# Expert stage: table entries read into registers in half turns inside the turn

## The chip, the cores and the metric

The kernel runs on one NeuronCore of a Trainium2 chip. The metric is the device time of one execution in microseconds (us); lower is better.

## The reference, cut to what matters

A two-layer block over 4 sequences of 512 rows of width 512. Layer 0 is a scan-based mixer and a Hadamard-rotated feed-forward layer; layer 1 is masked attention over a context of 1024 rows and then the part that matters here, a mixture of experts: each of the 2048 rows goes to the 8 best of 32 experts, and each expert is a gated feed-forward layer of inner width 192.

```python
router_logits = x2d @ gate_kernel                       # (2048, 32)
routing_weights = softmax(router_logits)
routing_weights, selected_experts = top_k(routing_weights, 8)
routing_weights = routing_weights / sum(routing_weights)
# for each expert e and the rows that chose it:
y = (silu(rows @ gate_proj[e]) * (rows @ up_proj[e])) @ down_proj[e]
# added to the row of the output, times its routing weight
```

## The kernel before

The earlier stages (mixer, feed-forward, attention, router) are straight code and loops that the change doesn't touch. The router sorts the rows by expert into a table in DRAM (`rows_by_expert`), each expert's rows padded to whole tiles of 128. That gives `NTILE` = 159 tiles. Which expert a tile belongs to is known only on the chip, so DVE computes an integer table `TAB` in SBUF, one column for each tile: row 0 is the tile's expert, row 1 the value at which its expert's rows are complete (`due`), row 2 the offset of its weights in the buffer `we`, row 3 its first row in `rows_by_expert`, row 4 the first tile of its expert.

The expert stage then runs over the tiles, one after the other, on five engines at once. It is written as a hardware loop `Fori` of `LOOPS` = 19 turns with `U` = 8 tiles unrolled in each, and a rest of 7 tiles (`REST`). For a tile t:

- ACT issues the gather of the tile's rows (`load_tile`, line 793, its DMA on line 798), `LEAD` = 6 tiles ahead, into one of 8 buffers.
- PE transposes the rows, two tiles ahead (`tile_transpose`, line 1698); ACT copies the high half (`tile_hi`, line 774, activation on line 777) and DVE computes the low half (`tile_lo`, line 1371).
- PE multiplies by gate and up, one tile ahead (`tile_up`, line 1708, twelve matmuls on lines 1471 to 1473); ACT takes the silu (`tile_silu`, line 779), DVE the product (`hidden`, lines 1382 and 1383).
- PE transposes the hidden rows (`hidden_transpose`, lines 1716 and 1717); ACT copies their high half (`hidden_hi`, line 783, activation on line 785), DVE the low half (`hidden_lo`, line 1378).
- PE multiplies by the down weights (`tile_down`, line 1719); DVE weighs the result (`weigh`, lines 1390 and 1391) and POOL adds it to the output by an indirect DMA (line 568). SP loads the experts' weights.

In each tile PE's order is: transposes of tile t+2, hidden transposes of t, gate and up of t+1, down of t. ACT's is: `hidden_hi(t)`, `tile_hi(t+2)`, the gather's DMA, `tile_silu(t+1)`. DVE's is: `hidden_lo(t)`, `tile_lo(t+2)`, `hidden(t+1)`, `weigh(t)`.

An address or a semaphore value that comes from the table must stand in a register of the engine that uses it. `load_ints` (line 92) takes fresh registers, fills them with one load instruction of the engine's own queue (line 95, TENSOR_LOAD in the trace) and turns them into values. Each engine does so at the top of a turn, right behind the loop's branch:

- PE: 12 entries of row 2 (line 1735).
- ACT: 12 entries of row 3, then 16 entries of row 1 (line 811), ahead of the first `hidden_hi`.
- DVE: 8 entries of row 0 (line 1397), ahead of the first `hidden_lo`.
- POOL: 8 entries of row 4, which the change leaves as it is.

Ahead of the loop and ahead of the rest each engine loads once more in the same way.

Of the kernel before, what the change touches and what calls it, by code (L numbers as in the profile page):

```python
# [22 lines left out]
P = 128  # L23
# [6 lines left out]
NE, M, TOPK = 32, 192, 8  # L30
# [5 lines left out]
E16 = EW + EL  # L36
# [6 lines left out]
CAP = NTOK + P  # L43
SPARES = 4
WP = 4
U = 8
LEAD = 6
V = U
LOOPS = NTILE // U
REST = NTILE - LOOPS * U  # L50
NEWTON = 13
# [40 lines left out]
def load_ints(eng, name, table, least, most):  # L92

    regs = [eng.alloc_register(f"{name}{i}") for i in range(table.shape[-1])]
    eng.reg_load(regs, table)  # L95
    return [eng.snap(x, donate=True, min_val=least, max_val=most) for x in regs]


def wait_apart(eng, sem, value, passed):
# [6 lines left out]
def build(nc, a_x, a_ctxT, a_ctxr, a_kv, a_mask, a_winT, a_woutT, a_cols, a_rows, a_wug, a_wdT,  # L106
          a_gk, a_exp, a_ident, a_had, a_hadf, a_tri, d_exp, d_kv, d_row, d_down, a_out):
    ctx = ExitStack()
    with ctx:
# [3 lines left out]
        def sem(name):  # L113
            return ctx.enter_context(nc.semaphore(name))
# [131 lines left out]
        o += U * RW  # L246
        yt = [BIG[:, o + i * D:o + (i + 1) * D] for i in range(V)]
        o += V * D
        xh = [f16(BIG, o + i * D // 2, (KC, P)) for i in range(2)]
# [22 lines left out]
        TAB = ex(5 * TABLE, I32, p=1).rearrange("p (a t) -> p a t", a=5)  # L272
        TCUM = ex(NE, I32, p=1)
        TODD = ex(TABLE, I32, p=1)
        TPAD = ex(NE, I32, p=1)
        IDY = ex(V, I32)

# [51 lines left out]
        s_xg = [sem(f"tile_gathered{i}") for i in range(U)]  # L329
        s_add = [sem(f"tile_added{i}") for i in range(V)]  # L330
        s_xt, s_xh, s_xl, s_ug, s_es, s_ea, s_at, s_ah2, s_al2, s_ed, s_y = (sem(n) for n in (
# [7 lines left out]
        def _(sp):  # L339
# [156 lines left out]
            with sp.Fori(1, NE // WP) as i:  # L496
                for h in range(WP):
# [5 lines left out]
                    load_expert(i * WP + h, h)  # L503
            for w in range(V):
                sp.wait_ge(s_add[w], 16 + 16 * (LOOPS + (w < REST)))


        @block.gpsimd
        def _(pool):
# [4 lines left out]
            pool.memset(SELS[:, :], 0.0).then_inc(s_ss, 1)  # L514
            for w in range(V):
                pool.dma_start(first[:, 2 * w:2 * w + 2], a_x[0:1, 2 * w:2 * w + 2]).then_inc(s_add[w], 16)
# [53 lines left out]

            with pool.Fori(0, LOOPS) as it:
                start = load_ints(pool, "expert_start", TAB[0:1, 4, bass.ds(it * U, U)], 0, NTILE)
# [3 lines left out]
            for u in range(REST):  # L576
                add(LOOPS * U + u, u, start[u])


        @block.scalar  # L580
        def _(act):
# [192 lines left out]
            def tile_hi(t, p, weights):  # L774
                act.wait_ge(s_wl, weights)
                act.wait_ge(s_xt, t + 1)
                act.activation(xh[p], PS[:, p, :].rearrange("p (k n) -> p k n", n=P), ACT.Copy, scale=H_S).then_inc(s_xh, 1)  # L777

            def tile_silu(t, p):
                act.wait_ge(s_ug, t + 1)  # L780
                act.activation(eg[p], PS[:, 2 + p, 0:M], ACT.Silu, scale=1.0 / (H_S * E_S)).then_inc(s_es, 1)  # L781

            def hidden_hi(t, p):
                act.wait_ge(s_at, t + 1)
                act.activation(eah[p], PS[:, 4, 0:2 * P], ACT.Copy).then_inc(s_ah2, 1)  # L785

            def rows_at(name, t, count):
                return load_ints(act, name, TAB[0:1, 3, bass.ds(t, count)], 0, NE * CAP + (SPARES - 1) * P)

            def experts_due(name, t, count):  # L790
                return load_ints(act, name, TAB[0:1, 1, bass.ds(t, count)], 16, 16 * NE)

            def load_tile(u, used, row, pads):

                act.wait_ge(s_pad, pads)
                if not isinstance(used, int) or used:
                    act.wait_ge(s_y, used)
                act.dma_start(xg[u], d_row[bass.ds(row, P), :]).then_inc(s_xg[u], 16)

            act.wait_ge(s_tab, 1)  # L800
            rows, due = rows_at("first_row", 0, U), experts_due("first_due", 0, U)
# [4 lines left out]
                load_tile(t, 0, rows[t], due[t])  # L806
            tile_hi(0, 0, due[0])
            tile_hi(1, 1, due[1])
            tile_silu(0, 0)
            with act.Fori(0, LOOPS) as it:  # L810
                rows, due = rows_at("tile_row", it * U + 4, U + 4), experts_due("tile_due", it * U, U + 8)
                for u in range(U):
                    t = it * U + u

                    hidden_hi(t, u % 2)
                    tile_hi(t + 2, u % 2, due[u + 2])
                    load_tile((u + LEAD) % U, t + (V + LEAD - U + 1), rows[u + LEAD - 4], due[u + LEAD])
                    tile_silu(t + 1, (u + 1) % 2)
            t = LOOPS * U
            rows, due = rows_at("last_row", t + LEAD, REST - LEAD), experts_due("last_due", t + 2, REST - 2)  # L820
            for u in range(REST):
                hidden_hi(t + u, u % 2)
                if u + 2 < REST:
# [8 lines left out]
        def _(dve):  # L832
# [538 lines left out]
            def tile_lo(t, p):  # L1371
                dve.wait_ge(s_xh, t + 1)
                v.scalar_tensor_tensor(xl[p], PS[:, p, :].rearrange("p (k n) -> p k n", n=P), H_S, xh[p],  # L1373
                                       ALU.mult, ALU.subtract).then_inc(s_xl, 1)
# [5 lines left out]
            def hidden(t, p):  # L1380
                dve.wait_ge(s_es, t + 1)
                v.scalar_tensor_tensor(ea[p][:, 0:M], PS[:, 2 + p, M:2 * M], 1.0 / (H_S * E_S), eg[p], ALU.mult, ALU.mult)  # L1382
                v.scalar_tensor_tensor(ea[p][:, M:2 * P], PS[:, 2 + p, M + P:2 * M], 1.0 / (H_S * E_S), eg[p][:, P:M],
                                       ALU.mult, ALU.mult).then_inc(s_ea, 1)
# [9 lines left out]
            tile_lo(1, 1)  # L1394
            hidden(0, 0)
            with dve.Fori(0, LOOPS) as it:
                experts = load_ints(dve, "tile_expert", TAB[0:1, 0, bass.ds(it * U, U)], 0, NE - 1)
                for u in range(U):
                    t = it * U + u
                    hidden_lo(t, u % 2)  # L1400
                    tile_lo(t + 2, u % 2)
                    hidden(t + 1, (u + 1) % 2)
                    weigh(t, u, it * (U // V) + u // V, experts[u])
            experts = load_ints(dve, "last_expert", TAB[0:1, 0, bass.ds(LOOPS * U, REST)], 0, NE - 1)
            for u in range(REST):
                t = LOOPS * U + u
                hidden_lo(t, u % 2)
                if u + 2 < REST:
                    tile_lo(t + 2, u % 2)
                if u + 1 < REST:  # L1410
                    hidden(t + 1, (u + 1) % 2)
                weigh(t, u, LOOPS * (U // V) + u // V, experts[u])
# [3 lines left out]
        def _(pe):  # L1416
# [287 lines left out]
            def weights_at(name, t, count):  # L1704

                return load_ints(pe, name, TAB[0:1, 2, bass.ds(t, count)], 0, (WP - 1) * E16)

            def tile_up(t, p, at):
                for k in range(KC):
                    hi = we[:, bass.ds(at + k * GU, GU)]  # L1710
                    lo = we[:, bass.ds(at + (EW + k * GU), GU)]
                    last = three(PS[:, 2 + p, 0:GU], xh[p][:, k, :], xl[p][:, k, :], hi, lo, k == 0, k == KC - 1)
                last.then_inc(s_ug, 1)
# [5 lines left out]
            def tile_down(t, p, at):  # L1719
                pe.wait_ge(s_al2, t + 1)  # L1720
                bank = PS[:, 5 + p, :]
                w0h, w1 = KC * GU, KC * GU + D
                hi, lo = we[:, bass.ds(at + w0h, D)], we[:, bass.ds(at + (EW + w0h), D)]
                stack = we[:, bass.ds(at + w1, D)]
                three(bank, eah[p][:, 0:P], eal[p][:, 0:P], hi, lo, True, False)

                mm(bank, eah[p][:, P:2 * P], stack, start=False, stop=False)  # L1727
                mm(bank, eal[p][:, P:2 * P], stack, start=False, stop=True).then_inc(s_ed, 1)  # L1728
# [1 line left out]
            tile_transpose(0, 0, 0)  # L1730
            tile_transpose(1, 1, 0)
            pe.wait_ge(s_xl, 1)
            tile_up(0, 0, weights_at("first_weights", 0, 4)[0])
            with pe.Fori(0, LOOPS) as it:
                at = weights_at("tile_weights", it * U, U + 4)
                for u in range(U):
                    t = it * U + u
                    tile_transpose(t + 2, (u + 2) % U, it + (u + 2) // U)


                    pe.wait_ge(s_ea, t + 1)
                    hidden_transpose(u % 2)
                    tile_up(t + 1, (u + 1) % 2, at[u + 1])
                    tile_down(t, u % 2, at[u])
            at = weights_at("last_weights", LOOPS * U, REST)
            for u in range(REST):
                t = LOOPS * U + u
                if u + 2 < REST:
                    tile_transpose(t + 2, (u + 2) % U, LOOPS + (u + 2) // U)
                pe.wait_ge(s_ea, t + 1)  # L1750
                hidden_transpose(u % 2)
                if u + 1 < REST:
                    tile_up(t + 1, (u + 1) % 2, at[u + 1])
                tile_down(t, u % 2, at[u])


# [66 lines left out]
```

## Time and profile before

| what | us |
|---|---|
| median of 3 runs (lowest, highest) | 1517.9 (1516.97, 1525.52) |
| the profiled execution | 1522.04 |
| its span, first to last instruction | 1520.2 |

The profiled execution lies 4.1 us above the median of the runs; 1.8 us of it are around the span. The trace gives times from the start of the span. An engine's name with a q behind it (ACTq, PEldq) is its instruction queue: loads into registers, branches, copies of registers, DMA issues. PE is the matmuls and PEld the loads of their weights, which overlap. Releasers are inferred, and an engine that isn't the bottleneck may be idle at no cost.

### The profile page before, as it was taken

How to read it: one execution, taken by the hardware profiler on the slowest of the kernel's cores; microseconds unless marked ns; L12 is line 12 of the kernel's file. 1: busy time of each engine (PE TensorE's matmuls, PEld its weight loads, DVE VectorE, ACT ScalarE, POOL GpSimd, SP SyncE). 2: the span in 40 equal slices, each digit the busy share in tenths (PEclk: the TensorE clock that was granted, in tenths of full speed). 3: DMA queues.
4: the chain of work that ended last, by engine and by line, in shares of the span. 5: the costliest groups of instructions: out<-in, count | busy, mean ns of one | idle time of the engine just before them, and what ended most of it. 6: DMA issues, size and time to landing. Idle time of an engine off the chain costs nothing.

```text
span 1520.2 us, 26971 instructions
## 1 busy us (share of the span) xinstructions
PE 1397.6 (92%) x7525; PEld 757.6 (50%) x7526; DVE 1026.8 (68%) x2471; ACT 505.1 (33%) x916; POOL 382.9 (25%) x313
## 2 busy tenths in 40 slices
PE   4599999999999999988989729999999999999997
PEld 3234444444444444444444315666666666666664
DVE  6848866985896546577776645666666666666664
ACT  1335444435334343332222103333333333333332
POOL 1000000000000000014546452344443334444443
PEclk9789999999999999999999959999999999999999
DMA  9955676767666678717665757889999989999886
GB/s 369 395 188 179 229 252 225 232 206 240 205 225 218 225 257 279 274 59 274 222 219 205 288 223 195 215 223 240 250 246 230 230 219 225 254 227 225 158 160 91
DMA packets 132696, 345.04 MB, mean 227 GB/s; under 512 B 15008, under 2 KB 19616, under 8 KB 125728
## 3 DMA queue, kind: packets, MB, share of 16 engines
q1 hardware_dynamic: 74528, 208.82, 40.8%
q0 software_dynamic: 34640, 85.74, 24.7%
q10 hardware_dynamic: 23472, 49.79, 10.3%
q8 instruction: 27, 0.44, 0.1%
q14 instruction: 29, 0.24, 0.0%
HBM read 192.68 MB, written 151.62 MB: 226 GB/s over the span
## 4 chain that ended last, share of the span: by engine, by line
PE 69%; DVE 12%; DMA 6%; issue 5%; another core or an unknown queue 3%; ACT 2%; SPq 2%; ACTq 1%; DVEq 0%; POOLq 0%
PE PS L1471 18%; PE PS L1473 18%; PE PS L1472 17%; PE PS L1701 4%; PE PS L1728 2%; PE PS L1727 2%; DMA split_experts<-HT 2%; DMA CST<-in_kv 2%; PE PS L1716 1%; PE PS L1717 1%; DMA BIG<-in_wdT 1%; PE PS L1429 1%; ACTq L95 1%; PE PS L1432 1%
## 5 line engine op out<-in xcount | busy, mean ns | idle before, releaser
L568 POOL DMA_INDIRECT out<-BIG,EX x159 | 247.1, 1554 | 360.9 <-DVE BIG L1391 185.2
L1471 PE MATMUL PS<-BIG 128*128 x795 | 268.3, 338 | 4.8 <-DVE BIG L1378 3.1
L1472 PE MATMUL PS<-BIG 128*128 x795 | 268.2, 337 | 0.0
L1473 PE MATMUL PS<-BIG 128*128 x795 | 268.2, 337 | 0.0
L1471 PE MATMUL PS<-HT,BIG 128*128 128x512 f16 (+1 forms) x512 | 196.6, 384 | 4.2 <-ACT EX L621 2.3
L1472 PE MATMUL PS<-HT,BIG 128*128 128x512 f16 (+1 forms) x512 | 196.1, 383 | 0.0
L1473 PE MATMUL PS<-HT,BIG 128*128 128x512 f16 (+1 forms) x512 | 196.0, 383 | 0.0
L546 POOL DMA_INDIRECT rows_by_expert<-HT,POS x128 | 124.3, 971 | 142.9 <-DVE POS L1276 108.4
L1471 PE MATMUL PS<-BIG,EX 128*128 128x512 f16 (+1 forms) x384 | 146.3, 381 | 6.6 <-DVE EX L1218 5.0
L1472 PE MATMUL PS<-BIG,EX 128*128 128x512 f16 (+1 forms) x384 | 146.2, 381 | 0.0
L1473 PE MATMUL PS<-BIG,EX 128*128 128x512 f16 (+1 forms) x384 | 146.0, 380 | 0.0
L785 ACT ACTIVATE BIG<-PS 128x256 f16<-128x256 f32 x159 | 60.9, 383 | 245.1 <-PE PS L1717 223.6
L1382 DVE SCALAR_TENSOR_TENSOR BIG<-PS,BIG 128x192 f32<-128x192 f32 x159 | 56.8, 357 | 104.4 <-ACT BIG L781 97.7
L1373 DVE SCALAR_TENSOR_TENSOR BIG<-PS,BIG 128x512 f16<-128x512 f32 x159 | 110.0, 692 | 21.1 <-ACT BIG L777 11.1
L1391 DVE TENSOR_SCALAR BIG<-PS,BIG 128x512 f32<-128x512 f32 x159 | 119.4, 751 | 0.0
L631 ACT ACTIVATE HT<-HT 128x1280 f16<-128x1280 f32 x64 | 81.1, 1268 | 97.3 <-DMA split_experts<-HT 97.3
L1701 PE MATMUL PS<-ident,BIG 128*128 128x128 f32 x636 | 96.7, 275 | 15.6 <-DMA BIG<-rows_by_expert 14.1
L540 POOL MEMSET HT<- 128x105 f32 x1 | 0.2, 185 | 425.9 <-DMA split_experts<-HT 425.9
L1473 PEld LDWEIGHTS PS<-BIG 128*128 128x128 f16 x795 | 78.0, 98 | 58.5 <-issue 0.3
L781 ACT ACTIVATE BIG<-PS 128x192 f32<-128x192 f32 x159 | 52.5, 330 | 158.1 <-PE PS L1473 133.3
L1701 PEld LDWEIGHTS PS<-ident,BIG 128*128 128x128 f32 x636 | 78.7, 142 | 48.9 <-issue 22.1
L1471 PEld LDWEIGHTS PS<-BIG 128*128 128x128 f16 x795 | 77.9, 98 | 50.2 <-issue 9.7
(239 smaller groups left out, 2240.5 us busy)
## 6 DMA issues: line engine op xcount, KB each, us to landing
BIG<-rows_by_expert ACTq DMA_DIRECT2D x159, 280.0 KB
HT<-in_experts SPq DMA_DIRECT2D x64, 640.0 KB, 4.8
BIG<-split_experts SPq DMA_DIRECT2D x32, 1152.0 KB
split_experts<-HT SPq DMA_DIRECT2D x96, 320.0 KB, 2.4
CST<-in_kv SPq DMA_DIRECT2D x64, 256.0 KB, 4.7
split_context<-RT SPq DMA_DIRECT2D x64, 256.0 KB, 4.5
BIG<-split_context SPq DMA_DIRECT2D x8, 2048.0 KB, 15.0
rows_by_expert<-X SPq DMA_DIRECT2D x32, 280.0 KB
```

What stands on the lines that cost most here:

```text
L546: pool.indirect_dma_start(d_row, bass.IndirectOffsetOnAxis(ap=POS[:, t % ZN, c:c + 1], axis=0), ZR[:, t % ZN, :], None).then_inc(s_ids[t % ...
L568: pool.indirect_dma_start(a_out, bass.IndirectOffsetOnAxis(ap=IDY[:, u % V:u % V + 1], axis=0), yt[u % V], None, compute_op=ALU.add).then_ ...
L631: act.activation(eoh, est[h], ACT.Copy, scale=E_S).then_inc(s_eh, 1)
L781: act.activation(eg[p], PS[:, 2 + p, 0:M], ACT.Silu, scale=1.0 / (H_S * E_S)).then_inc(s_es, 1)
L785: act.activation(eah[p], PS[:, 4, 0:2 * P], ACT.Copy).then_inc(s_ah2, 1)
L1373: v.scalar_tensor_tensor(xl[p], PS[:, p, :].rearrange("p (k n) -> p k n", n=P), H_S, xh[p], ALU.mult, ALU.subtract).then_inc(s_xl, 1)
L1382: v.scalar_tensor_tensor(ea[p][:, 0:M], PS[:, 2 + p, M:2 * M], 1.0 / (H_S * E_S), eg[p], ALU.mult, ALU.mult)
L1391: v.tensor_scalar(yt[u % V], PS[:, 5 + u % 2, :], xg[u][:, bass.ds(e + D, 1)], None, ALU.mult).then_inc(s_y, 1)
L1471: mm(out, lh, rh, start=first, stop=False)
L1472: mm(out, lh, rl, start=False, stop=False)
L1473: return mm(out, ll, rh, start=False, stop=last_group)
L1701: last = nc.tensor.transpose(PS[:, u % 2, k * P:(k + 1) * P], xg[u][:, k * P:(k + 1) * P], ident[:, :])
```

## The change

On PE, ACT and DVE no register load stands at the top of a turn any more. PE and ACT keep registers that outlive the turn (`at_regs`, `row_regs`, `due_regs`); they are filled ahead of the loop for the first turn, and late in each turn for the next one. At the top of the turn their contents are copied into values (`values`, which keeps the registers for the next load).

- PE: 4 entries are copied at the top; 4 more are loaded behind `tile_down` of the turn's tile 1; behind `tile_down` of tile 5 the 4 of the next turn are loaded, and the first of them is copied at once, since tile 7 needs it.
- ACT: 4 rows and 8 due values are copied behind `hidden_hi` of tile 0; behind the gather's DMA and ahead of `tile_silu`, 4 rows are loaded in tile 2, 8 due values in tile 3, 4 rows of the next turn in tile 6, 8 due values of the next turn in tile 7.
- DVE: the 8 experts are loaded behind `tile_lo` of tile 0, ahead of `hidden`.

Engine work, its order, the waits and the DMAs are the same ones.

```diff
@@ -46,6 +46,7 @@
 U = 8
 LEAD = 6
 V = U
+H = U // 2
 LOOPS = NTILE // U
 REST = NTILE - LOOPS * U
 NEWTON = 13
@@ -94,6 +95,11 @@
     regs = [eng.alloc_register(f"{name}{i}") for i in range(table.shape[-1])]
     eng.reg_load(regs, table)
     return [eng.snap(x, donate=True, min_val=least, max_val=most) for x in regs]
+
+
+def values(eng, regs, least, most):
+
+    return [eng.snap(x, min_val=least, max_val=most) for x in regs]
 
 
 def wait_apart(eng, sem, value, passed):
@@ -784,8 +790,10 @@
                 act.wait_ge(s_at, t + 1)
                 act.activation(eah[p], PS[:, 4, 0:2 * P], ACT.Copy).then_inc(s_ah2, 1)
 
+            ROW_MOST = NE * CAP + (SPARES - 1) * P
+
             def rows_at(name, t, count):
-                return load_ints(act, name, TAB[0:1, 3, bass.ds(t, count)], 0, NE * CAP + (SPARES - 1) * P)
+                return load_ints(act, name, TAB[0:1, 3, bass.ds(t, count)], 0, ROW_MOST)
 
             def experts_due(name, t, count):
                 return load_ints(act, name, TAB[0:1, 1, bass.ds(t, count)], 16, 16 * NE)
@@ -806,18 +814,33 @@
                 load_tile(t, 0, rows[t], due[t])
             tile_hi(0, 0, due[0])
             tile_hi(1, 1, due[1])
+            row_regs = [act.alloc_register(f"turn_row{i}") for i in range(H)]
+            due_regs = [act.alloc_register(f"turn_due{i}") for i in range(U)]
+            act.reg_load(row_regs, TAB[0:1, 3, LEAD:LEAD + H])
+            act.reg_load(due_regs, TAB[0:1, 1, 2:2 + U])
             tile_silu(0, 0)
             with act.Fori(0, LOOPS) as it:
-                rows, due = rows_at("tile_row", it * U + 4, U + 4), experts_due("tile_due", it * U, U + 8)
                 for u in range(U):
                     t = it * U + u
 
                     hidden_hi(t, u % 2)
-                    tile_hi(t + 2, u % 2, due[u + 2])
-                    load_tile((u + LEAD) % U, t + (V + LEAD - U + 1), rows[u + LEAD - 4], due[u + LEAD])
+                    if u == 0:
+                        rows, due = values(act, row_regs, 0, ROW_MOST), values(act, due_regs, 16, 16 * NE)
+                    elif u == H:
+                        rows, due = later_rows, later_due
+                    tile_hi(t + 2, u % 2, due[u % H])
+                    load_tile((u + LEAD) % U, t + (V + LEAD - U + 1), rows[u % H], due[u % H + LEAD - 2])
+                    if u == H - 2:
+                        later_rows = rows_at("later_row", it * U + (H + LEAD), H)
+                    elif u == H - 1:
+                        later_due = experts_due("later_due", it * U + (H + 2), U)
+                    elif u == U - 2:
+                        act.reg_load(row_regs, TAB[0:1, 3, bass.ds(it * U + (U + LEAD), H)])
+                    elif u == U - 1:
+                        act.reg_load(due_regs, TAB[0:1, 1, bass.ds(it * U + (U + 2), U)])
                     tile_silu(t + 1, (u + 1) % 2)
             t = LOOPS * U
-            rows, due = rows_at("last_row", t + LEAD, REST - LEAD), experts_due("last_due", t + 2, REST - 2)
+            rows, due = values(act, row_regs, 0, ROW_MOST), values(act, due_regs, 16, 16 * NE)
             for u in range(REST):
                 hidden_hi(t + u, u % 2)
                 if u + 2 < REST:
@@ -1394,19 +1417,21 @@
             tile_lo(1, 1)
             hidden(0, 0)
             with dve.Fori(0, LOOPS) as it:
-                experts = load_ints(dve, "tile_expert", TAB[0:1, 0, bass.ds(it * U, U)], 0, NE - 1)
                 for u in range(U):
                     t = it * U + u
                     hidden_lo(t, u % 2)
                     tile_lo(t + 2, u % 2)
+                    if u == 0:
+                        experts = load_ints(dve, "tile_expert", TAB[0:1, 0, bass.ds(it * U, U)], 0, NE - 1)
                     hidden(t + 1, (u + 1) % 2)
                     weigh(t, u, it * (U // V) + u // V, experts[u])
-            experts = load_ints(dve, "last_expert", TAB[0:1, 0, bass.ds(LOOPS * U, REST)], 0, NE - 1)
             for u in range(REST):
                 t = LOOPS * U + u
                 hidden_lo(t, u % 2)
                 if u + 2 < REST:
                     tile_lo(t + 2, u % 2)
+                if u == 0:
+                    experts = load_ints(dve, "last_expert", TAB[0:1, 0, bass.ds(LOOPS * U, REST)], 0, NE - 1)
                 if u + 1 < REST:
                     hidden(t + 1, (u + 1) % 2)
                 weigh(t, u, LOOPS * (U // V) + u // V, experts[u])
@@ -1705,6 +1730,14 @@
 
                 return load_ints(pe, name, TAB[0:1, 2, bass.ds(t, count)], 0, (WP - 1) * E16)
 
+            at_regs = [pe.alloc_register(f"turn_weights{i}") for i in range(H)]
+
+            def next_weights(t):
+                pe.reg_load(at_regs, TAB[0:1, 2, bass.ds(t, H)])
+
+            def first_weights(count):
+                return values(pe, at_regs[:count], 0, (WP - 1) * E16)
+
             def tile_up(t, p, at):
                 for k in range(KC):
                     hi = we[:, bass.ds(at + k * GU, GU)]
@@ -1730,9 +1763,10 @@
             tile_transpose(0, 0, 0)
             tile_transpose(1, 1, 0)
             pe.wait_ge(s_xl, 1)
-            tile_up(0, 0, weights_at("first_weights", 0, 4)[0])
+            pe.reg_load(at_regs, TAB[0:1, 2, 0:H])
+            tile_up(0, 0, first_weights(1)[0])
             with pe.Fori(0, LOOPS) as it:
-                at = weights_at("tile_weights", it * U, U + 4)
+                at = first_weights(H)
                 for u in range(U):
                     t = it * U + u
                     tile_transpose(t + 2, (u + 2) % U, it + (u + 2) // U)
@@ -1742,7 +1776,12 @@
                     hidden_transpose(u % 2)
                     tile_up(t + 1, (u + 1) % 2, at[u + 1])
                     tile_down(t, u % 2, at[u])
-            at = weights_at("last_weights", LOOPS * U, REST)
+                    if u == 1:
+                        at += weights_at("later_weights", it * U + H, H)
+                    elif u == U - 3:
+                        next_weights(it * U + U)
+                        at += first_weights(1)
+            at = first_weights(H)
             for u in range(REST):
                 t = LOOPS * U + u
                 if u + 2 < REST:
@@ -1752,6 +1791,8 @@
                 if u + 1 < REST:
                     tile_up(t + 1, (u + 1) % 2, at[u + 1])
                 tile_down(t, u % 2, at[u])
+                if u == 1:
+                    at += weights_at("last_weights", t + (H - 1), REST - H)
 
 
 def kernel(x, ctx_2048, mask_BxS2_bk0, L0_xattn_decay, L0_xattn_W_in, L0_xattn_b_in, L0_xattn_W_out,
```

## Rows read from the trace of the kernel before

**Rows 1.** The page, part 1: busy time of each engine.

```profile
PE 1397.6 (92%) x7525; PEld 757.6 (50%) x7526; DVE 1026.8 (68%) x2471; ACT 505.1 (33%) x916; POOL 382.9 (25%) x313
```

**Rows 2.** Stretch: us, busy PE, PEld, DVE, ACT, POOL, clock, DMA share, GB/s.

```profile
920.81:1509.02 588.21, 584.30 (x3628) 368.83 (x3627) 389.44 (x946) 188.98 (x473) 244.01 (x157) 1.00 0.88 214
```

**Rows 3.** The chain that ended last, by time: start us, us, what.

```profile
924.18 0.44 PE PS L1701 x4
...
946.28 0.44 PE PS L1701 x4
949.97 0.44 PE PS L1701 x4
953.65 0.44 PE PS L1701 x4
...
1064.42 0.44 PE PS L1701 x4
...
1067.45 1.55 ACTq L95
1069.11 1.59 ACTq L95
...
1073.05 0.44 PE PS L1701 x4
...
1154.46 0.44 PE PS L1701 x4
...
1162.43 0.44 PE PS L1701 x4
...
1501.96 0.44 PE PS L1701 x4
```

**Rows 4.** Line 95, whole run: duration ns min/median/max, first and last start.

```profile
L95 ACTq TENSOR_LOAD <-EX x42: 293/1020/1850, 903.8 to 1486.4; - x42
L95 PEldq TENSOR_LOAD <-EX x21: 517/872/1568, 915.5 to 1485.5; - x21
...
L95 DVEq TENSOR_LOAD <-EX x20: 603/609/1683, 920.3 to 1487.4; - x20
```

**Rows 5.** Line 95 at three turn boundaries (at 948.7, 1066.9 and 1156.9 us).

```profile
L95 ACTq TENSOR_LOAD <-EX x2: 783/902/1020, 949.3 to 950.2; - x2
L95 PEldq TENSOR_LOAD <-EX x1: 862/862/862, 948.7 to 948.7; - x1
...
L95 ACTq TENSOR_LOAD <-EX x2: 1547/1570/1592, 1067.5 to 1069.1; - x2
L95 PEldq TENSOR_LOAD <-EX x1: 1107/1107/1107, 1066.9 to 1066.9; - x1
...
L95 PEldq TENSOR_LOAD <-EX x1: 1440/1440/1440, 1156.9 to 1156.9; - x1
```

**Rows 6.** A tile of the stage in order of time, ACT, DVE and PE.

```profile
1035.74 0.59 ACT L777 ACTIVATE BIG<-PS 128x512 f16<-128x512 f32 x1
...
1036.37 0.69 DVE L1373 SCALAR_TENSOR_TENSOR BIG<-PS,BIG 128x512 f16<-128x512 f32 x1
...
1037.41 0.33 ACT L781 ACTIVATE BIG<-PS 128x192 f32<-128x192 f32 x1 [1.08 <-PE PS L1473]
...
1037.78 0.36 DVE L1382 SCALAR_TENSOR_TENSOR BIG<-PS,BIG 128x192 f32<-128x192 f32 x1 [0.72 <-ACT BIG L781]
...
1038.05 0.21 DVE L1383 SCALAR_TENSOR_TENSOR BIG<-PS,BIG 128x64 f32<-128x64 f32 x1
...
1038.66 0.14 PEld L1716 LDWEIGHTS PS<-ident,BIG 128*128 128x128 f32 x1
```

**Rows 7.** Lines 798 and 1734: a register copy, a gather's issue, the branch of PE.

```profile
L798 ACTq MOVE BIG<-rows_by_expert x159: 29/29/29, 909.1 to 1488.6; - x159
L798 ACTq DMA_DIRECT2D BIG<-rows_by_expert x159: 338/339/402, 909.1 to 1488.6; - x159
...
L1734 PEldq COMPARE_BRANCH  x19: 83/215/225, 948.3 to 1485.4; - x19
```

## The prediction, made before the changed kernel had run

> **What bounds the kernel now.** I read the page first: TensorE (PE) is busy in 92% of the span, no other engine above 68% [rows 1]. The change touches the expert stage alone, so the next view is that stretch: from the first hidden transpose to the last are 588.21 us, PE is busy in 584.30 of them at a granted clock of 1.00, which is 2.4 GHz, and DVE in 389 [rows 2]. So PE bounds the stage, and what there is to win is the time in which it is short of instructions. The chain in order of time gives the beat. The four row transposes (line 1701) mark each tile: from 924.18 to 946.28 us lie 6 tiles, 22.10 us, so 3.684 us a tile [rows 3]. From 924.18 to 1501.96 us lie 155 tiles; at that beat they would take 571.0 us and they take 577.8 [rows 3]. The whole loss of the stage's steady part is thus **6.8 us**, 0.45% of the kernel. Nothing the change touches can bring more than this, unless it shortens the beat, and it leaves PE's work as it is.
>
> Where do the 6.8 us stand? At the turn boundaries, and in few of them. Around the first (loads from 948.7 us) the beats are 3.69 and 3.68: nothing is lost [rows 3]. There ACT's two loads took 0.78 and 1.02 us, PE's 0.86 [rows 5]. Around the boundary at 1067 us two tiles take 8.63 us instead of 7.37, 1.26 lost, and the chain names ACT's loads, now 1.55 and 1.59 us [rows 3]. Around 1157 us two tiles take 7.97, 0.60 lost [rows 3]; there PE's load took 1.44 us [rows 5]. So the loads of usual length are just hidden, and only slow ones show:
> - ACT's pair hides 3.14 - 1.26 = 1.88 us; the usual pair, 1.80, fits.
> - PE's load hides 1.44 - 0.60 = 0.84 us, and the usual 0.86 fits to within 0.02.
> Over the run ACT's loads reach 1.85 us and PE's 1.57, with medians of 1.02 and 0.87 [rows 4]. That is a cover at its edge: it holds for a usual load and for no slower one.
>
> **The change, part by part.** A load's price grows with its registers. ACT's take 0.78 us for 12 and 1.02 for 16 [rows 5], 0.06 a register; the shortest, a load of a single register ahead of the rest, takes 0.29 [rows 4]. PE's shortest, of 4 registers, takes 0.52; DVE's of 8 are 0.61 in the median [rows 4]. So I take 0.45 to 0.52 us for 4 registers and 0.61 for 8. The slowest over the median is 1.8 for ACT and PE and 2.8 for DVE (1.683 over 0.609) [rows 4]; I keep 1.8 as the usual bad case, 2.8 as the outer one.
>
> ACT removes 1.80 us of loads in front of `hidden_hi`. The new loads stand between the gather's issue and `tile_silu`. In the tile of [rows 6] `tile_hi` starts at 1035.74, the issue takes 0.34 [rows 7], and silu starts at 1037.41, waiting for PE: 1.3 us of waiting queue. A load of 0.61 us fits, and at 1.8 times as well (1.1). At 2.8 times (1.7) silu is 0.4 late; the product behind it ends at 1038.26 and PE's hidden transposes begin loading at 1038.66 [rows 6], so 0.4 more is covered. Cost nothing, at the outer end below 0.1 a turn.
>
> ACT adds 12 register copies behind `hidden_hi` in tile 0. A copy takes 0.029 us [rows 7], so 0.35 us, part of it under `hidden_hi` itself. `tile_hi` then starts up to 0.35 later, and `tile_lo`, which here runs from 1036.37 to 1037.06, ends before the 1037.78 of DVE's next product [rows 6]. The gather's issue moves with it, but it is six tiles ahead. Nothing. If the values were taken without copies it is nothing as well.
>
> PE removes 12 registers at the branch (0.87) and keeps the branch, 0.22 [rows 7], and adds 4 copies, 0.12. The two loads inside the turn, 4 registers each, stand behind `tile_down`, where PE's queue is as far ahead as at the boundary, and without the branch: cover at least 0.84 + 0.22 us. At 0.52 they fit, and at 1.8 times (0.94) too. Cost nothing; bounds: a small gain that the beat itself can't show, and, were no cover there at all, 38 x 0.52 = 19.8 us. I take nothing, since the load of 0.86 at the boundary is covered.
>
> DVE's load leaves the place ahead of `hidden_lo`. This matters, since with ACT on time it would have become late itself. In its new place it has from the start of `tile_lo`, 1036.37, to 1037.78, 1.4 us, and 0.4 before PE waits [rows 6]; the slowest, 1.68, fits.
>
> No load is moved past a DMA of SP or POOL; ACT's gathers keep their order, and those at a turn's top start earlier by the removed loads. Ahead of the loop ACT now loads 4 and 8 registers in front of the first silu. That silu waits for PE's first twelve matmuls and the table load of the activation; 1.1 us lies inside this wait. The last turn and the rest gain like the others.
>
> What is late next? Nothing before PE itself: the beat of 3.684 holds at each boundary. Leftover: the branch with copies, and rare loads of the outer kind, together 0.3 us. **Sum: -6.8 + 0.3 = -6.5 us**, from 1522.0 to 1515.5 for the profiled execution.
>
> This execution lies 4.1 us above the median of 1517.9, and the fastest run is at 1517.0. If slow loads are as common in a run without profile, the median falls by 6.5, to 1511.4. If the runs' spread is itself made by slow loads, the median run lost only 6.8 - 4.1 = 2.7 and falls to about 1515.3. I take the middle, **1513.5**.
>
> The Trainium skill speaks on both prices. Its page "Runtime: NRT & Kernel Launch", section "Instruction fetch mechanics", puts a register load at about 200 ns a register; by that an 8-register load would be an estimated 1.6 us and would outlast ACT's 1.3. The loads of 12 and 16 registers here differ by 0.06 us a register [rows 5], so the trace disagrees and decides.
>
> **The rivals.**
> - *No loss in an unprofiled run* (chance 0.22). The slow loads might come from the profile's own traffic. For it: the profiled run is above the median, and usual loads lose nothing. Against: one run is at 1525.5 without any profile. Then the change brings 0 to 1: 1517.5.
> - *The branch is the stall* (0.05). If the return to the turn's top is what costs, the loads only fill a time that is lost anyway, and 6.5 us stay: 1517.9. Against it: boundaries with quick loads lose nothing, and PE's branch takes 0.22 at most [rows 3, 7]. The same section of the Trainium skill says that a taken branch whose target is out of the fetched window stalls; no row here shows it.
> - *PE's loads come into view* (slower, 0.07). Behind `tile_down` of tiles 1 and 5 PE's queue must be ahead. If it isn't, because the transposes' weights for the next tile must be issued in that time, each load shows whole: 38 x 0.52 = 19.8, less 6.8: +13, 1531. It decides from 0.18 us of uncovered load upwards (6.8 / 38). For it: the cover at the boundary, 0.84, is close to the load there. Against: the load is 0.3 shorter now. By over 1% slower only if all were slow as well (38 x 0.94 = 35.7, +29).
> - *The loads get slower in their new places* (0.06). They now stand in the midst of the weights' DMAs, four for ACT instead of two. With half of the loss left, 3.4: 1514.5 to 1517; inside the range.
>
> **How the numbers follow.** Forecast 0.60, rivals 0.22, 0.05, 0.07, 0.06. About 1%, 15 us, is what a measurement of this kernel can tell from no change. The forecast and three rivals lie within it wholly, the slower one mostly. Faster by over 1%: 0.02, since even 6.8 us is less than half of it. Slower: 0.02. The same: 0.96. The range goes from 1509.5, the full gain with a quiet base, to 1519.0, no gain with some drift.
>
> **What would show it.** In the changed profile: a beat of 3.68 us across all 19 boundaries; line 95 gone from the chain between 920 and 1500 us; loads of PE 4 registers near 0.5 us, of ACT 0.45 and 0.6, begun before silu's start; silu's and the product's idle time unchanged; a stage of 582 us. PE's idle weight loads ending in "issue" behind tiles 1 and 5 would show the slower rival; a late first transpose at the boundary with no load near it, the branch. I am wrong if the stage still takes over 585 us, or if the stage is shorter and the median isn't.

## The result, and the profile after

The changed kernel is slower: a median of 1540.95 us of 4 runs (1538.8 to 1543.24), against 1520.83 for the kernel before beside it. The ratio is 1.0131, with a 95% interval of 1.0094 to 1.0169. The prediction had 1513.5 us, with a range up to 1519.0.

The first lines of the page of the changed kernel:

```profile
span 1538.9 us, 27126 instructions
...
PE 1408.3 (92%) x7525; PEld 761.6 (49%) x7526; DVE 1021.8 (66%) x2471; ACT 507.3 (33%) x916; POOL 383.0 (25%) x313
```

The span has grown by 18.7 us, and PE's share of it has hardly changed [rows 1]. The stretch from the first to the last recorded hidden transpose (length, busy PE, PEld, DVE, ACT, POOL, clock, DMA share, GB/s):

```profile
920.72:1520.77 600.05, 584.28 (x3589) 365.85 (x3589) 379.42 (x936) 189.47 (x468) 240.88 (x155) 1.00 0.87 209
```

It is 600.05 us now, though it is two tiles short of the stretch before [rows 2], and so beyond the 585 us that the prediction named as its sign of being wrong; the clock granted is again 1.00. Between the first and the last regular set of row transposes lie the same 155 tiles in both kernels. They take 596.4 us (924.02 to 1520.39 in the chain below) where they took 577.8 [rows 3], that is 25.3 us over a beat of 3.684 instead of 6.8. So the whole difference of 18.6 us is in the steady part of the expert stage, as idle time of PE. The chain in order of time shows what makes it (start us, us, what):

```profile
924.02 0.44 PE PS L1726 x4
...
976.96 0.44 PE PS L1726 x4
978.40 1.98 ACTq L840
984.80 0.44 PE PS L1726 x4
988.48 0.44 PE PS L1726 x4
...
993.62 3.66 ACTq L96
1001.70 0.44 PE PS L1726 x4
...
1025.71 2.65 ACTq L96
...
1520.39 0.44 PE PS L1726 x4
```

From 976.96 to 984.80 two tiles take 7.84 us, 0.47 too much, with a load of line 840 of 1.98 us between them. From 988.48 to 1001.70 three tiles take 13.22, 2.17 too much, with a load of 3.66 us. The loads of ACT have not left the chain [rows 3]; they stand in it in most half turns, and each of the 38 half turns loses at least 0.25 us. Their durations (ns, min/median/max):

```profile
L96 ACTq TENSOR_LOAD <-EX x40: 547/1648/3658, 903.6 to 1488.2; - x40
...
L96 DVEq TENSOR_LOAD <-EX x20: 601/606/1321, 922.2 to 1507.3; - x20
L96 PEldq TENSOR_LOAD <-EX x20: 329/335/947, 926.1 to 1511.3; - x20
...
L838 ACTq TENSOR_LOAD <-EX x19: 917/991/2371, 944.2 to 1499.5; - x19
...
L840 ACTq TENSOR_LOAD <-EX x19: 1762/1935/3719, 948.3 to 1503.2; - x19
```

Line 96 is the helper's: on ACT the loads of 4 and of 8 in the middle of the turn, and the two at the head; lines 838 and 840 are the loads for the next turn, of 4 and of 8 registers. Before, ACT's load of 12 took 783 ns and that of 16 took 1020 [rows 5]. Now a load of 4 takes 917 at the least and one of 8 takes 1762. PE's loads of 4 are quick, 335 in the median, and DVE's of 8 take 606 as they did [rows 4]. One tile of the changed kernel in order of time shows how the load is felt:

```profile
1025.22 0.59 ACT L783 ACTIVATE BIG<-PS 128x512 f16<-128x512 f32 x1
...
1025.26 0.34 ACTq L806 DMA_DIRECT2D BIG<-rows_by_expert  x1
...
1028.41 0.33 ACT L787 ACTIVATE BIG<-PS 128x192 f32<-128x192 f32 x1 [2.59 <-issue]
...
1029.05 0.21 DVE L1406 SCALAR_TENSOR_TENSOR BIG<-PS,BIG 128x64 f32<-128x64 f32 x1
...
1029.31 0.14 PEld L1749 LDWEIGHTS PS<-ident,BIG 128*128 128x128 f32 x1 [1.18 <-DVE BIG L1406]
```

The gather's issue (ACTq) stands beside the copy on line 783, then the load of 2.65 us from the chain follows, at 1025.71, and silu (line 787) starts at 1028.41, 3.2 us behind the copy instead of 1.7 [rows 6]. The product on line 1406 and PE's hidden transposes (line 1749) follow it, and PE's weight loads have been idle for 1.18 us.

### The profile page after: what moved, and what is told of

Same layout as the page of the kernel before. It is cut to its first block, busy times and chain, and to the rows that moved or that the text cites. A ratio compares the mean times of both kernels' runs of the same rounds, so it can differ in the third digit from the quotient of the medians.

```text
span 1538.9 us, 27126 instructions
## 1 busy us (share of the span) xinstructions
PE 1408.3 (92%) x7525; PEld 761.6 (49%) x7526; DVE 1021.8 (66%) x2471; ACT 507.3 (33%) x916; POOL 383.0 (25%) x313
## 3 DMA queue, kind: packets, MB, share of 16 engines
q0 software_dynamic: 34640, 85.74, 24.7%
## 4 chain that ended last, share of the span: by engine, by line
PE 63%; DVE 13%; DMA 6%; ACTq 6%; issue 5%; ACT 4%; another core or an unknown queue 2%; SPq 1%; DVEq 0%; POOLq 0%
PE PS L1498 16%; PE PS L1496 16%; PE PS L1497 16%; ACTq L96 3%; PE PS L1726 3%; ACTq L840 2%; DMA split_experts<-HT 2%; PE PS L1761 2%; PE PS L1760 2%; DMA CST<-in_kv 2%; PE PS L1749 2%; DVE BIG L1414 1%; DMA BIG<-in_wdT 1%; PE PS L1454 1%
## 5 line engine op out<-in xcount | busy, mean ns | idle before, releaser
L1496 PE MATMUL PS<-BIG,EX 128*128 128x512 f16 (+1 forms) x384 | 147.9, 385 | 8.4 <-DVE EX L1241 6.7
L1498 PE MATMUL PS<-BIG,EX 128*128 128x512 f16 (+1 forms) x384 | 147.8, 385 | 0.0
L1497 PE MATMUL PS<-BIG,EX 128*128 128x512 f16 (+1 forms) x384 | 147.7, 385 | 0.0
L1498 PEld LDWEIGHTS PS<-BIG 128*128 128x128 f16 x795 | 78.0, 98 | 60.1 <-issue 0.5
L783 ACT ACTIVATE BIG<-PS 128x512 f16<-128x512 f32 x159 | 94.2, 593 | 19.5 <-PE PS L1726 19.5
```

What stands on the lines that cost most here:

```text
L1496: mm(out, lh, rh, start=first, stop=False)
L1497: mm(out, lh, rl, start=False, stop=False)
L1498: return mm(out, ll, rh, start=False, stop=last_group)
```

## The experiments

A look at the addresses gave the theory. The rows of the table `TAB` are 168 entries of 4 bytes apart and its start is a multiple of 16 bytes into its buffer. The loads before begin at entries 8i (PE, DVE, ACT's due values) or 8i + 4 (ACT's rows), all multiples of 16 bytes. ACT's new loads begin at 8i + 10 and 8i + 14 (rows) and 8i + 6 and 8i + 10 (due values), all 8 bytes past such a multiple. PE's and DVE's new loads begin at multiples. **Theory A**: a load from a multiple of 16 bytes reads four entries at a time, one from elsewhere reads them singly. This is inferred: what the traces show are durations, and they fit 0.08 us + 0.235 for each four, or 0.08 + 0.21 for each one. The rivals were that ACT's own DMA issue just ahead makes the load slow (B), the activation beside it (C), or the registers that it fills (D).

**The table's rows moved to where the new loads are aligned.** The changed kernel with this one edit, which shifts rows 1 and 3 by 8 bytes and rows 0, 2 and 4 by a multiple of 16:

```diff
-        TAB = ex(5 * TABLE, I32, p=1).rearrange("p (a t) -> p a t", a=5)
+        TAB = ex(5 * (TABLE + 2), I32, p=1).rearrange("p (a t) -> p a t", a=5)[:, :, 0:TABLE]
```

> The changed kernel with the rows of the integer table 170 entries apart instead of 168, so that ACT's loads of 4 and 8 entries begin at a multiple of 4 entries (16 bytes), as PE's and DVE's always did; nothing else moves. Theory A (a register load whose address is not a multiple of 16 bytes reads its entries one by one, 0.21 us each; an aligned one reads four at a time, 0.235 us): ACT's loads of 4 take about 0.32 us instead of 0.92, those of 8 about 0.55 instead of 1.76; no loss at tiles 3 and 7; the 26 us that the stage loses fall to under 1; about 1513 to 1516 us, faster than both kernels. Rival B (the load is slow because it stands right behind ACT's own DMA issue): loads stay at 0.92 and 1.76, time stays at 1540. Rival C (it is slow because an activation is running beside it): the same as B. Rival D (it is slow because of which registers it fills): the same as B.

Measured: 1481.23 us against 1488.01 for the kernel before on the same chip, which is faster by itself than the first one; ratio 0.9952 (0.9935 to 0.9969). The loads of 4 and of 8 registers for the next turn, same places and same registers:

```profile
L838 ACTq TENSOR_LOAD <-EX x19: 310/315/1063, 909.6 to 1440.1; - x19
...
L840 ACTq TENSOR_LOAD <-EX x19: 542/551/1342, 913.3 to 1443.8; - x19
```

They fell from 917 and 1762 ns at the least to 310 and 542, and the 155 tiles lose 0.03 us. B, C and D are out: places, counts and registers are the same, and the address of the loads changed. (The small buffers behind `TAB` moved with it, by 40 bytes; the prices further down show the same durations with nothing moved.)

The padding has a price elsewhere: it misaligns ACT's two loads of 8 ahead of the loop. They took 3.27 and 3.15 us here, against 1.03 and 0.55 in the changed kernel. Theory A gives 1.76; why these two last longer is open. No delay followed: the first row transposes came 10.9 us after the start of the first of these loads, and 10.8 in the next run of the changed kernel on this chip, whose rows aren't padded (ACT's loads behind silu, below).

**The kernel before with its loads misaligned.** The same edit of the table on the kernel before, where it puts ACT's two loads at 8 bytes past a multiple.

> The kernel before with the table's rows 170 entries apart instead of 168, so that ACT's two loads at the top of a turn begin at 8 bytes past a multiple of 16. Theory A: the load of 12 registers goes from 0.79 us to 0.08 + 12 x 0.21 = 2.6, that of 16 from 1.02 to 3.4; together 6.0 against 1.88 that are covered, so 4.1 us lost at each of 19 boundaries, 78 us, about 1595 us. Rivals B, C and D: the loads stay at 0.79 and 1.02, about 1520.

Measured: 1614.82 us, one run, 127 above the median of the kernel before. The chain at one boundary:

```profile
1135.37 2.60 ACTq L95
...
1138.08 3.43 ACTq L95
...
1144.06 0.42 PE PS L1727
```

The loads last 2.60 and 3.43 us, as worked out. The time rose by more than the 78 us expected. One part is that many of the pairs were slower still, as in the kernel before, with loads up to 4.89 us; another part is PE's clock, which fell at PE's pause at 17 of the 18 boundaries among the 155 tiles. The stretches before and behind this boundary (length, busy PE, PEld, DVE, ACT, POOL, clock, DMA share, GB/s):

```profile
1125.00:1135.00 10.00, 10.00 (x66) 6.43 (x65) 6.95 (x16) 3.30 (x9) 4.74 (x4) 1.00 0.99 256
1143.00:1148.00 5.00, 5.00 (x18) 2.90 (x17) 2.63 (x7) 0.87 (x2) 2.77 (x2) 0.50 1.06 194
```

The clock granted was 1.00 before PE's pause and 0.50 behind it, so a matmul on line 1727 took 0.42 us of the chain where it usually takes 0.22. The trace tells how the loss divides. The 155 tiles lose 128.3 us. The 18 pairs of loads among them last 92.2 us beyond the 1.88 that are covered, where 18 times 4.1, 74, were expected. PE was busy for 71.9 us at a clock of 0.50 behind these pauses, which costs half of it, 36.0 us. The two make 128.2. At the one boundary where the clock stayed at 1.00, at 1029.7 us, the loss was 4.65 us and the pair lasted 4.64 beyond 1.88.

**What a load costs by count and address**, first try.

> The kernel before with one more load on ACT behind the gather's issue of tiles 0 to 6 of each turn, into registers that nothing reads: 4 registers from a multiple of 4 entries, 4 from one past it, 4 from two past it, 8 aligned, 8 from two past, 1 aligned, 6 aligned. Theory A: least durations of 0.32, 0.92, 0.92, 0.55, 1.76, 0.29 us, and the 6 something between 0.55 and 1.3. Rival B (place behind the DMA issue) and C (running activation): 0.92, 0.92, 0.92, 1.76, 1.76 and 0.3, whatever the address.

The build left the loads out, since nothing read their registers: the program had the 26971 instructions of the kernel before, and no durations came of it. It is a repeat of the kernel before instead, 1485.4 us, with 6.3 us lost over the 155 tiles on this chip.

**ACT's loads behind silu.** The changed kernel with `tile_silu` ahead of the four loads, away from ACT's DMA issue:

```diff
                     load_tile((u + LEAD) % U, t + (V + LEAD - U + 1), rows[u % H], due[u % H + LEAD - 2])
+                    tile_silu(t + 1, (u + 1) % 2)
                     if u == H - 2:
...
                         act.reg_load(due_regs, TAB[0:1, 1, bass.ds(it * U + (U + 2), U)])
-                    tile_silu(t + 1, (u + 1) % 2)
```

> The changed kernel with ACT's four loads of a turn moved from between the gather's issue and tile_silu to behind tile_silu, where no DMA of ACT was issued for over a us; addresses as changed. Theory A: the loads still take at least 0.92 and 1.76 us. Behind silu the queue has about 1.7 us until hidden_hi and 0.75 more are covered (the two loads of before hid 1.88), so only the slow ones show: about 2 to 5 us of loss, 1518 to 1522 us. Rival B: the loads take 0.32 to 0.45 and 0.55 to 0.61, and the stage loses nothing, about 1515.

Measured: 1489.1 us, one run, against 1488.0 for the kernel before; the 155 tiles lose 12.5 us. The loads of 4 and of 8 for the next turn:

```profile
L839 ACTq TENSOR_LOAD <-EX x19: 917/1365/1917, 906.4 to 1448.7; - x19
...
L841 ACTq TENSOR_LOAD <-EX x19: 1744/2017/4538, 910.1 to 1452.4; - x19
```

Away from the DMA issue they are no quicker, which speaks against B once more. The place has more cover, so half of the loss is gone, though less than I had expected: I had left out how often the loads are slowed beyond their least duration.

**The prices again**, on the kernel before, with a wait that keeps each load:

```diff
+                    if u == 0:
+                        act.reg_load(probe[:4], TAB[0:1, 1, bass.ds(it * U, 4)])
+                        act.wait_ge(s_wl, act.snap(probe[2], min_val=16, max_val=16 * NE))
+                    elif u == 1:
+                        act.reg_load(probe[:4], TAB[0:1, 1, bass.ds(it * U + 1, 4)])
...
```

> The kernel before with one more load on ACT behind the gather's issue of tiles 0 to 6 of each turn, and behind each a wait on one of its entries that is met already, so that the load is kept: 4 registers from a multiple of 4 entries, 4 from one past it, 4 from two past it, 8 aligned, 8 from two past, 1 aligned, 6 aligned. Theory A (aligned loads read four entries at a time): least durations 0.31, 0.92, 0.92, 0.54, 1.76, 0.29 us; for the 6, open: one read of four and then two single ones would be 0.08 + 0.235 + 2 x 0.21 = 0.74, two reads of four 0.55, six single ones 1.34. Rival (only offsets of two entries are slow, or only the number of registers counts): the 4 from one past would be 0.31. The time itself: the load of 8 from two past is beyond its cover of 1.5 us, 0.3 to 0.5 us at 19 turns, 5 to 10 us above the kernel before.

The lines of the seven loads, in the order of the expectation:

```profile
L820 ACTq TENSOR_LOAD <-EX x19: 312/313/869, 890.4 to 1443.0; - x19
...
L823 ACTq TENSOR_LOAD <-EX x19: 907/923/1814, 893.4 to 1446.0; - x19
...
L826 ACTq TENSOR_LOAD <-EX x19: 907/926/2414, 897.0 to 1449.7; - x19
...
L829 ACTq TENSOR_LOAD <-EX x19: 539/560/1443, 900.6 to 1453.3; - x19
...
L832 ACTq TENSOR_LOAD <-EX x19: 1752/1788/3256, 904.3 to 1456.9; - x19
...
L835 ACTq TENSOR_LOAD <-EX x19: 290/293/734, 908.3 to 1460.9; - x19
...
L838 ACTq TENSOR_LOAD <-EX x19: 757/787/2271, 912.0 to 1464.6; - x19
```

Least durations of 312, 907, 907, 539, 1752, 290 and 757 ns, against 310, 920, 920, 540, 1760, 290 expected, and for the 6 aligned ones 740, one read of four and two single ones. An offset of one entry is as bad as one of two. One entry costs 0.29 us, four aligned ones 0.31. An offset of three was not tried. The kernel took 1505.54 us, 18.6 above the one before, more than the 5 to 10 expected: the tiles with the load of 8 from two past lose 10.9 us over the run, those with the two loads of 4 that aren't aligned 2.9, and the last two tiles of the turns 8.7, against 6.3 in the repeat of the kernel before.

**Why were usual loads sometimes slow before?** In the trace of the kernel before, 25 of the 76 loads that PE, ACT and DVE issue in the turns last over 1.15 times their least duration. Of these 25, 20 overlap one of POOL's indirect DMA instructions, and of the other 51, 15 do. So POOL's adds were taken out, and the adding to the output with them:

```diff
-                pool.indirect_dma_start(a_out, bass.IndirectOffsetOnAxis(ap=IDY[:, u % V:u % V + 1], axis=0), yt[u % V], None,
-                                        compute_op=ALU.add).then_inc(s_add[u % V], 16)
+                pool.sem_inc(s_add[u % V], 16)
```

> The kernel before without POOL's indirect DMA of each tile: the expert layer's results are computed and never added to the output, and the small loads that seed their semaphores are increments. Theory P (the slow register loads at some turn boundaries of the kernel before come from POOL's indirect DMAs beside them): PE's loads of 12 stay at 0.85 to 0.90, ACT's at 0.79 and 1.02 with none above 1.1, DVE's at 0.61; the steady part of the expert stage loses under 1 us instead of 6 to 7. Rival (they come from the weights' and gathers' DMAs): several loads of 1.1 to 1.8 us stay, and so do 3 us or more of the loss.

Measured: 1479.66 us, one run, and 1.8 us lost over the 155 tiles instead of 6.3.

```profile
L95 ACTq TENSOR_LOAD <-EX x42: 297/1012/1826, 866.4 to 1446.9; - x42
L95 PEldq TENSOR_LOAD <-EX x21: 522/849/1617, 880.3 to 1446.0; - x21
...
L95 DVEq TENSOR_LOAD <-EX x20: 596/603/1081, 885.6 to 1447.9; - x20
```

The medians are the usual durations, but the maxima are not under 1.1 us: at two of the 19 boundaries PE's load took 1.62 and 1.17 us and ACT's first load, of 12, took 1.56 and 1.83. At these two, and at no other, SP had issued the DMA of an expert's weights 2.3 us ahead of PE's load and a second DMA 0.8 to 0.9 ahead; at six others it issued the weights' DMA some 6 us ahead, and no load was slow. So the loads slow down without POOL's DMAs in 5 of 76 cases instead of 25. That SP's DMAs make the rest is a guess from two boundaries, and whether it is the issue of a DMA or its traffic that slows a load, no run here tells. The expectation that none would be above 1.1 failed.

**PE's and DVE's parts alone**, with ACT's loads at the top of the turn as before.

> The changed kernel with ACT's loads as before, all at the top of the turn: the parts of PE and DVE alone. Each boundary then loses what ACT's pair lasts beyond 1.88 us, which is most of what it lost before (only boundaries where PE's load alone was slow gain): 0 to 2 us under the kernel before, ratio 0.999 to 1.000. If the parts of PE or DVE cost anything (the slower rival of the prediction, 13 us), it is 1.009.

Measured: 1487.56 us against 1486.9, ratio 1.0006 (0.9992 to 1.0019): no difference.

```profile
L96 ACTq TENSOR_LOAD <-EX x42: 295/1018/2061, 868.0 to 1452.1; - x42
...
L96 PEldq TENSOR_LOAD <-EX x20: 329/334/1179, 893.1 to 1458.3; - x20
```

PE's loads of 4 are at 334 ns, out of the chain, and the 155 tiles lose 5.5 us. ACT's pair makes 4.3 of them, at four boundaries. At the last of the four DVE's load was late as well, in its new place, behind a pair of 2.87 us; the chain names it, and the boundary lost 0.9 us more than the pair explains:

```profile
1420.65 1.02 ACTq L96
...
1421.78 1.85 ACTq L96
...
1424.76 1.67 DVEq L96
```

**ACT's part alone, aligned**, with PE and DVE as before.

> ACT's part of the change alone, with the table's rows 170 entries apart so that its loads are aligned; PE and DVE load at the top of the turn as before. What is lost is then what PE's load of 12 lasts beyond 0.85 us: about 3 us of the 6.5. Ratio about 0.997 to 0.998, between the kernel before and the changed kernel with aligned rows (0.995).

Measured: 1481.69 us against 1486.9, ratio 0.9975 (0.9962 to 0.9987), with 4.5 us lost over the 155 tiles, more than the 3 expected. What is left stands at the boundaries where PE's load was slow:

```profile
L96 PEldq TENSOR_LOAD <-EX x21: 521/906/1822, 877.2 to 1445.3; - x21
```

**The changed kernel and its aligned version side by side**, on one chip.

> The changed kernel once more, on the chip of the next run, so that the two stand side by side. Theory A: it loses at each turn what its load of 8 lasts beyond the 1.5 us of its cover, at tiles 3 and 7: at least 38 x 0.26 = 10 us and with slow loads some 20 to 26, against the 6 to 7 of the kernel before; ratio 1.010 to 1.014.

Measured: 1538.22 us against 1519.79, ratio 1.0113 (1.009 to 1.0137), and 24.7 us lost over the 155 tiles.

> The changed kernel with the table's rows 170 entries apart, again: ratio 0.995 as in its first run, loads of 4 and 8 at 0.31 and 0.54 us, no loss at any tile of the expert stage.

Measured: 1514.0 us, ratio 0.9953 (0.9932 to 0.9973). The chain of this run:

```profile
928.17 0.44 PE PS L1726 x4
931.85 0.44 PE PS L1726 x4
...
1127.11 0.44 PE PS L1726 x4
```

From 931.85 to 1127.11 lie 53 tiles and six turn boundaries, in 195.26 us: 3.684 a tile, with nothing lost. All 155 tiles lose 0.3 us. Two entries of padding between the rows of a table are worth 24 us to the changed kernel, and this version beats both.

## Why the prediction was wrong

**The step that failed is the price of ACT's loads**: "I take 0.45 to 0.52 us for 4 registers and 0.61 for 8". The loads of 4, 8, 12 and 16 from which I took it all began at multiples of 16 bytes, and I priced by count alone. (The single register of 0.29 us came from elsewhere, but one entry costs 0.29 from an aligned address as well.) In ACT's new places the price is 0.92 and 1.76. A load of 8 then outlasts its cover at tiles 3 and 7 of each turn. The rest follows by the prediction's own way of reckoning: the cover was 1.50 us (1.98 - 0.47 and 3.66 - 2.17 in the chain above), so 38 loads of 8 lose at least 38 x 0.26 = 9.9 us. With the slow ones among them, up to 3.72 us, they last 22.9 us beyond 1.50 in all, and the slow loads of 4 last 2.3 beyond it. That is 25.1 of the 25.3 lost.

**Rows that could have warned me.** In [rows 4] ACT's longest load is 1850 ns, and it started last, at 1486.4 us: that is not a load of 16 but the one of 5 due values ahead of the rest, line 820, which begins two entries past a multiple. By theory A it costs 0.08 + 5 x 0.21 = 1.13 us undisturbed. In the run without POOL's adds it took 1.12. I had read this row as the slow end of one population. DVE's longest, 1683 ns, is no load of 8 either but the one of 7 ahead of the rest: in the run without POOL's adds it took 1.08 against 0.60 for 8, so the factor of 2.8 over the median mixed two counts. And PE's 0.52 for 4 registers was a single load ahead of the loop; it lasts as long after the change (0.51), while the loads of 4 in the turns take 0.33. A row's least and its maximum should have been led back to their places in the code before they were used as a price and a spread.

**The page's figure was dismissed too soon.** The Trainium skill's "Runtime: NRT & Kernel Launch", section "Instruction fetch mechanics", gives about 200 ns a register. The runs agree with it for loads that aren't aligned, 0.21 us; aligned ones took 0.235 for four. I set the figure aside on rows of the second kind. The estimate of 1.6 us for the load of 8 that follows from the page's figure was close to the 1.76 measured.

**The rivals.** The one that came true is "the loads get slower in their new places", which I gave 0.06 and, as its price, half of the loss (3.4 us left); its mechanism was not DMA traffic but the address, and 25.3 us were lost. The slower rival named PE's queue, and there nothing is lost: tiles 1 and 5 keep the beat, and PE's part with DVE's alone gives 1.0006. "No loss in an unprofiled run" is refuted, since the aligned version gains 0.5% in the median of 6 and again of 5 runs, and not in the profiled execution alone. "The branch is the stall" is refuted too, since the aligned version keeps each branch and the beat.

**What held.** The 6.8 us over the beat were all there was to win; once the loads are aligned, 0.0 to 0.3 us of them are left and the kernel is 5.8 to 6.8 us faster, against the sum of 6.5. PE's loads are hidden behind `tile_down`, DVE's usual loads of 0.60 behind `tile_lo`, and the copies of registers are not seen: ACT's 12 take 0.22 us at the top of a turn, where I had put 0.35. ACT's cover, 1.3 + 0.4 = 1.7 by my reckoning, measured 1.50. DVE's, 1.4 + 0.4, measured 1.40: in the last run its first load in the loop took 1.59 us, and the tile lost 0.19. So "the slowest, 1.68, fits" did not hold, at 0.2 us, and 0.9 where ACT was late too.

**The chances.** I gave 0.02 to slower by over 1%, because I bounded every load by durations of its own engine and let the place vary only in how much it covers. The outer bound of a load's price should have been open to what an address may change.

## What to carry to other kernels

Begin a register load at a multiple of 16 bytes: 8 entries cost 0.54 us then, and 1.76 from an address that isn't one. Let the count be a multiple of 4: on DVE an aligned load of 8 took 0.60 us and one of 7 took 1.07. When a table is read at a new offset, pad its rows so that the new offset is aligned; that is one line, but look at which other loads it misaligns. And look at the chain after such a move: a load that was harmless at the top of a turn, with 1.9 us of cover, isn't so ahead of an activation, with 1.5.

## What the runs showed of the hardware

- A load of registers on ACT took 0.08 us and 0.235 for each four entries when it began at a multiple of 16 bytes in the buffer (4, 8, 12 and 16 entries: 0.31, 0.54, 0.78, 1.02 us), and 0.08 us and 0.21 for each entry when it began elsewhere (4, 8, 12, 16: 0.91, 1.75, 2.60, 3.43). A rest of two entries behind a group of four costs what two single ones do (6 entries: 0.76, against 0.74 by that sum). PE and DVE took nearly the same for aligned loads (PE 4: 0.33, 12: 0.85; DVE 8: 0.60); loads that aren't aligned were run on ACT alone.
- It doesn't wait for the engine: moved behind silu, it started 0.09 us after silu's start, while silu (0.33 us) was running. Nor does a DMA issue ahead of it matter: its least durations stayed at 0.92 and 1.74 us.
- Loads are slowed at times, up to 3.4 times (1063 ns for 4 aligned entries, against 310). With POOL's indirect DMAs left out this happened to 5 loads of 76 instead of 25, and 1.8 us were lost instead of 6.3.
- When PE paused for 4.0 us, waiting for a pair of ACT's loads of 6.0 us in all, the clock granted was 1.00 (2.4 GHz) before the pause and 0.50 (1.2 GHz) for 5.6 us behind it. In the changed kernel, whose half turns lose up to 2.2 us each, it stayed at 1.00 throughout the stage.
